# Local attention and feed-forward with other pieces: norms spread as three bf16 pieces, feed-forward from f16 halves, probabilities normalized before their transpose, v held in the array

## What is computed

```python
def attn_layer(x, Wqkv, qs, ksc, Wo):
    q, k, v = heads(x @ Wqkv)                       # 16 heads of 64
    q, k = l2norm(q) * qs, l2norm(k) * ksc
    q = q * cos * scale + rotate_half(q) * sin * scale
    k = k * cos / scale + rotate_half(k) * sin / scale
    # windows of 32 queries see their own and the window before, masked to i-32 <= j <= i
    attn = softmax(8 * q @ k.T + mask)
    return (attn @ v) @ Wo

def ffn_layer(x, g, bln, W1, b1, W2, b2):
    xn = layernorm(x) * g + bln
    a, gate = split(xn @ W1 + b1)                   # 341 and 341
    return a * gelu(gate) @ W2 + b2

for i in range(6):
    x = attn_layer(shift(x), ...) + x
    x = ffn_layer(shift(x), ...) + x
```

## Time and profile before

| | |
|---|---|
| median of 3 runs | 3942.01 us (3941.55 to 3944.91) |
| the profiled execution, its span | 3944.5 us |
| PE busy | 3691.1 us, 94% of the span |
| PEld busy | 2146.6 us, 54% |
| DVE busy | 2985.9 us, 76% |
| ACT busy | 2392.9 us, 61% |
| POOL busy | 2310.3 us, 59% |
| DMA, busy share of 16 engines | 37.4% in the queue of the data |

### The profile page before, as it was taken

How to read it: one execution, slowest core, us unless ns; L and a number is a source line. 1 busy time by engine, 2 the same in 40 slices (tenths; PEclk the granted TensorE clock), 3 DMA queues, 4 the chain that set the end, 5 groups by cost and what they waited for, 6 DMA issues and landing times.

```text
span 3944.5 us, 165118 instructions
## 1 busy us (share of the span) xinstructions
PE 3691.1 (94%) x73780; PEld 2146.6 (54%) x73780; DVE 2985.9 (76%) x3451; ACT 2392.9 (61%) x2931; POOL 2310.3 (59%) x1892
## 2 busy tenths in 40 slices
PE   7999998799999999999999999999999999999996
PEld 4666665455555555555555455555555555555553
DVE  7888886677777777777777677777777777777774
ACT  6777776455656655566555565555565656666652
POOL 4555654666655666656666565656565655666651
PEclk9999999899999999999999999999999999999998
DMA  1000001444444444445354444444444444444442
GB/s 59 5 5 7 5 5 39 106 100 111 101 101 104 108 108 104 101 95 123 89 121 95 97 103 108 108 107 96 109 112 109 101 101 103 110 103 106 101 101 77
DMA packets 162073, 349.17 MB, mean 89 GB/s; under 512 B 32606, under 2 KB 41948, under 8 KB 155100
## 3 DMA queue, kind: packets, MB, share of 16 engines
q1 hardware_dynamic: 161372, 338.62, 37.4%
HBM read 24.54 MB, written 4.19 MB: 7 GB/s over the span
## 4 chain that ended last, share of the span: by engine, by line
PE 66%; issue 5%; DMA 4%; ACT 3%; SPq 2%; DVE 2%; POOL 1%; ACTq 0%; DVEq 0%; POOLq 0%
PE psB L677 32%; PE psA L677 26%; DMA vev<-vo 3%; PE psA L732 3%; PE psB L758 2%; PE psB L732 2%; ACT pb L1015 1%; PE psA L758 1%; ACT vo L1007 1%; SPq L502 1%; SPq L486 1%; SPq L504 1%; DMA kf<-h 1%; DVE h L1253 0%; ACT sq L985 0%
## 5 line engine op out<-in xcount | busy, mean ns | idle before, releaser
L1354 POOL TENSOR_TENSOR sq<-sq 128x512 f32<-128x512 f32 x384 | 490.1, 1295 | 492.6 <-ACT sq L985 492.3
L1349 POOL TENSOR_TENSOR h<-h,ts 128x512 f32<-128x512 f32 x384 | 490.3, 1277 | 211.1 <-DVE ts L1245 211.1
L1329 POOL TENSOR_TENSOR pt<-wk,pt 128x256 f16<-128x256 f32 (+3 forms) x256 | 368.0, 1453 | 286.6 <-ACT pt L908 196.9
L1350 POOL TENSOR_TENSOR h<-h,ts 128x512 f32<-128x512 f32 x384 | 489.6, 1275 | 0.0
L985 ACT ACTIVATE sq<-psA 128x1024 f32<-128x1024 f32 x240 | 245.7, 1024 | 168.3 <-PE psA L677 168.2
L1237 DVE TENSOR_TENSOR h<-psA,t_rot 128x1024 f32<-128x1024 f32 x240 | 293.0, 1221 | 38.1 <-ACT sq L985 17.3
L677 PE MATMUL psB<-vev,ptb 64*32 64x65 f32 x9216 | 244.4, 225 | 59.0 <-ACT pb L1015 35.2
L1245 DVE TENSOR_TENSOR ts<-psA,t_rot 128x1024 f32<-128x1024 f32 x240 | 291.6, 1215 | 3.1 <-POOL h L1350 3.1
L677 PEld LDWEIGHTS psB<-vev,ptb 64*32 64x32 f32 x9216 | 194.7, 106 | 175.5 <-issue 103.3
L1364 POOL TENSOR_SCALAR f_a<-f_a 128x512 f32<-128x512 f32 x48 | 31.2, 650 | 401.6 <-DVE f_a L1293 401.6
L1253 DVE TENSOR_TENSOR h<-h,psB 128x1024 f32<-128x1024 f32 x192 | 229.5, 1217 | 42.4 <-PE psB L677 40.3
(11 more groups left out here) (343 smaller groups left out, 10637.5 us busy)
## 6 DMA issues: line engine op xcount, KB each, us to landing
qf<-h SPq DMA_DIRECT2D x768, 136.0 KB, 2.5
kf<-h SPq DMA_DIRECT2D x768, 136.0 KB
vev<-vo SPq DMA_DIRECT2D x192, 260.0 KB, 4.1
vev<-vo SPq DMA_DIRECT2D x192, 227.5 KB, 4.6
stage<-wqk SPq DMA_DIRECT2D x12, 512.0 KB, 4.6
stage<-wvl SPq DMA_DIRECT2D x12, 256.0 KB, 5.3
stage<-wof SPq DMA_DIRECT2D x6, 512.0 KB, 5.1
xb<-xt SPq DMA_DIRECT2D x8, 256.0 KB, 8.1
```

Source lines behind the costliest of these rows:

```text
L1329: e.tensor_tensor(pt[g][pr][:, :, 1, o:o + w], wk[(slot_of(s)[0] - 1) % SLOTS][:, :, 0:w], pt[g][pr][:, :, 0, o:o + w], ALU.subtract).then ...
L1349: e.tensor_tensor(halves_of(h, 0), halves_of(h, 0), t[1], ALU.subtract)
L1350: e.tensor_tensor(halves_of(h, 1), halves_of(h, 1), t[0], ALU.add).then_inc(ended["ad"])
L1354: e.tensor_tensor(sqb[c][:, 0, :], sqb[c][:, 0, :], sqb[c][:, 1, :], ALU.add).then_inc(ended["qa"])
```

## The change

It edits the local stage; the causal stage only gets its masks from another place in a table.

1. **Norms.** After nw, ACT copies n_a rounded to bf16 (ca), DVE subtracts that from groups of rows (cs), ACT copies again (cb) and DVE subtracts again (ct). Tile n_b in bf16 then holds three pieces of each norm in three groups of rows, and bc is a bf16 matmul of n_b with a `spread` that sums the three.
2. **Feed-forward.** f_c, f_g and the weights are split into high and low f16 halves. f and fo are three f16 matmuls each where they were one f32. New steps: fh (ACT) and fl (POOL) split f_c, gh (ACT) and gl (DVE) split the products. `first_halves` and `second_halves` split the weights on DVE once for each layer. The bias b2 becomes a last row of w2. The load of the next layer's weights moves from the third half of its own layer to the ninth half of the layer before.
3. **Probabilities.** DVE sums them and takes the reciprocal (sm), POOL multiplies (pn) before tp. There are two tiles for them (pbs). v loses its column of ones.
4. **pv.** v (64 columns) is loaded into the array and the transposed probabilities (32 columns) move through it. The result comes out with channels on the partitions, the kinds nm and ot are gone, and the two pv steps of an rp share one PSUM tile.
5. **Orders.** All five strings are new. `with_first` puts a few first steps ahead of the lists. The DMA scratch of GpSimd becomes 1024.

```diff
 GPSIMD = (
-    "lx qa10 ad10 qa11 qa13 qa12 ad11 xl+1 ad13 nw1 ad12 qa01+1 ad01+1 ad00+1 qa00+1 qa03+1 qa02+1 ad03+1 nw0+1 "
-    "ad02+1 "
+    "qa01 ad01 qa00 qa03 qa02 xl ad00 ad03 nw0 qa12 ad02 pn00 ad12 qa13 pn01 qa11 qa10 ad13 lx nw1 fl ad11 pn10 ad10 "
+    "pn11 "
 )
...
 TENSOR = (
...
+    "sc000:A+1 sc011+1 sc003+1 sc002+1 sc001+1 pj12:A+1 ng01+1 ng00+1 op:B bc00:B+1 vp01:A+1 vp00:A+1 bc01:B+1 la:A+1 "
+    "pj13:B+1 tp00:A+1 lb:B+1 pj11:A+1 pj10:A+1 pv000:B+1 pv001+1 tp01:B+1 ss1:A+1 fo:B sc100:B+1 pv010:A+1 sc103+1 "
+    "sc101+1 sc102+1 pv011+1 sc110:B+1 ng10+1 sc111+1 sc113+1 sc112+1 vp11:A+1 vp10:A+1 bc11:B+1 bc10:A+1 ng11+1 "
+    "pj01:A+2 tp10:B+1 f0:B+1 pv100:B+1 pv101+1 pj00:A+2 tp11:B+1 f1:A+1 pj03:B+2 pj02:B+2 f2:A+1 pv110:A+1 pv111+1 "
+    "ss0:A+2 sc010:B+2 sc013+2 sc012+2 "
...
+def with_first(steps, *first):
+
+    return list(first) + [s for s in steps if s not in first]
...
                 elif kind == "pv":
                     rp, th = s[2:]
...
+                    o = psum(("pv", v, rp, 0))
                     for tq in range(2):
-                        for x in range(2):
-                            for g in range(4):
-                                t = 2 * th + tq
-                                vals = vo[v % 2] if g % 2 else vev
+                        for g in range(4):
+                            t = 2 * th + tq
+                            vals = vo[v % 2] if g % 2 else vev
+                            for x in range(2):
                                 for q in range(2):
-                                    at = 512 * q + 65 * (2 * tq + x)
-                                    rows = slice(64 * q, 64 * q + 64)
-                                    p = mm(o[32 * g:32 * g + 32, at:at + 65], ptb[rows, x, t, 32 * g:32 * g + 32],
-                                           vals[rows, 2 * t + g // 2, 2 * rp + x, :], tile_position=(64 * q, 32 * g))
+                                    rows, at = slice(64 * q, 64 * q + 64), 512 * q + 128 * t + 32 * g
+                                    p = mm(o[64 * x:64 * x + 64, at:at + 32], vals[rows, 2 * t + g // 2, 2 * rp + x, :],
+                                           ptb[rows, x, t, 32 * g:32 * g + 32], tile_position=(64 * q, 64 * x))
...
-                        p = mm(o[:, 512 * x:512 * x + 512], spread[rows, :], n_a[rows, :], tile_position=(64 * k + 32 * x, 0))
+                        p = mm(o[:, 512 * x:512 * x + 512], spread[rows, :], n_b[rows, :], tile_position=(64 * k + 32 * x, 0))
...
-                        p = mm(o[0:n, 512 * x:512 * x + 512], w1r[:, FF * x + 128 * j:FF * x + 128 * j + n], f_c[:, :])
+                        at = FF * x + 128 * j
+                        oy = o[0:n, 512 * x:512 * x + 512]
+                        mm(oy, w1s[1][:, at:at + n], f_ch[:, :], True, False)
+                        mm(oy, w1s[0][:, at:at + n], f_cl[:, :], False, False)
+                        p = mm(oy, w1s[0][:, at:at + n], f_ch[:, :], False, True)
...
+                elif kind == "ca":
+                    e.wait_ge(*done("nw", v))
+                    e.activation(n_c[:, :], n_a[:, :], ACT.Copy).then_inc(ended["ca"])
...
+        def first_halves(e, li):
+
+            e.wait_ge(s_w1, 16 * (li + 1))
+            g = t_gs[:, li:li + 1]
+            e.tensor_scalar(w1s[0][:, :], w1r[:, :], g, None, ALU.mult).then_inc(s_w1h)
+            e.wait_ge(s_w1h, li + 1)
+            e.scalar_tensor_tensor(out=w1s[1][:, :], in0=w1r[:, :], scalar=g, in1=w1s[0][:, :], op0=ALU.mult,
+                                   op1=ALU.subtract).then_inc(s_w1s)
...
+                elif kind == "cs":
+                    e.wait_ge(*done("ca", v))
+                    e.scalar_tensor_tensor(out=n_a[:, :], in0=n_c[:, :], scalar=less[:, 0:1], in1=n_a[:, :], op0=ALU.mult,
+                                           op1=ALU.add).then_inc(ended["cs"])
...
+                elif kind == "sm":
+                    rp = s[2]
+                    if v:
+                        e.wait_ge(*done("pn", v - 1, rp))
+                    e.wait_ge(*done("ex", v, rp))
+                    e.tensor_reduce(sums[rp][:, :], pbs[rp].rearrange("p x t (f s) -> p (x t f) s", f=2), AXX, ALU.add).then_inc(s_rc)
+                    e.wait_ge(s_rc, count[s])
+                    e.reciprocal(rc[rp][:, :], sums[rp][:, :]).then_inc(ended["sm"])
...
+                elif kind == "gl":
+                    j = s[2]
+                    n = FP[j]
+                    e.wait_ge(*done("gh", v, j))
+                    e.tensor_tensor(f_gl[j][0:n, :], f_g[j][0:n, :], f_gh[j][0:n, :], ALU.subtract).then_inc(ended["gl"])
...
+                elif kind == "pn":
+                    rp = s[2]
+                    w = pbs[rp].rearrange("p x t (f s) -> p (x t f) s", f=2)
+                    e.wait_ge(*done("sm", v, rp))
+                    e.tensor_tensor(w, w, rc[rp][:, :].unsqueeze(2).to_broadcast([128, 16, 2 * W]), ALU.mult).then_inc(ended["pn"])
...
+                elif kind == "fl":
+                    e.wait_ge(*done("fh", v))
+                    e.tensor_tensor(f_cl[:, :], f_c[:, :], f_ch[:, :], ALU.subtract).then_inc(ended["fl"])
```

More of the change, by code:

```diff
@@ L27 @@
 WS = 64.0
+WF = 8.0
 TINY = WS * WS * 1e-24
@@ L242, in flat @@
             return t.rearrange("p a b -> p (a b)")
-        t_mats = sb("t_mats", [128, 384 + 160])
-        ident, center, mean, spread, heads = (t_mats[:, a:z] for a, z in ((0, 128), (128, 256), (256, 384), (384, 512),
-                                                                           (512, 544)))
-        t_masks = sb("t_masks", [128, 384 + 2 * W], BF16)
+        t_mats = sb("t_mats", [128, 384 + W + 2])
+        ident, center, mean, heads, less = (t_mats[:, a:z] for a, z in ((0, 128), (128, 256), (256, 384), (384, 416), (416, 418)))
+        t_masks = sb("t_masks", [128, 384 + 2 * W + 128], BF16)
         identb = t_masks[:, 0:128]
@@ L252, in program @@
         keyid = t_masks[:, 384:384 + 2 * W]
+        spread = t_masks[:, 384 + 2 * W:384 + 2 * W + 128]
         t_scl = sb("t_scl", [128, L, 4])
@@ L316, in program @@
         n_r, n_a = (sb("n_" + x, [128, S]) for x in "ra")
-        vo = [sb(f"vo{n}", [128, 8, 4, 65]) for n in range(2)]
-        vev = sb("vev", [128, 8, 4, 65])
-        pb = sb("pb", [128, 2, NT, 2 * 2 * W])
+        n_c, n_b = (sb("n_" + x, [128, S], BF16) for x in "cb")
+        vo = [sb(f"vo{n}", [128, 8, 4, DH]) for n in range(2)]
+        vev = sb("vev", [128, 8, 4, DH])
+        pbs = [sb(f"pb{n}", [128, 2, NT, 2 * 2 * W]) for n in range(2)]
         ptb = sb("ptb", [128, 2, NT, 128])
         negm = [sb(f"negm{n}", [128, 16], BF16) for n in range(2)]
-        rc = [sb(f"rc{n}", [128, 2, 4]) for n in range(2)]
-        ob = sb("ob", [128, 2, 2, 2, 128])
+        sums, rc = ([sb(f"{x}{n}", [128, 16]) for n in range(2)] for x in ("sum", "rc"))
         ot2 = [sb(f"ot{z}", [128, 2, 2, 2, S], F16) for z in "hl"]
@@ L326, in program @@
         f_g = [sb(f"f_g{j}", [128, S]) for j in range(3)]
+        f_ch, f_cl = (sb("f_c" + z, [128, S], F16) for z in "hl")
+        f_gh, f_gl = ([sb(f"f_g{z}{j}", [128, S], F16) for j in range(3)] for z in "hl")
+        w1s = [sb("w1" + z, [128, 2 * FF], F16) for z in "hl"]
+        w2s = [sb("w2" + z, [128, 3, 128], F16) for z in "hl"]
+        t_gs = sb("t_gs", [128, L])
         x1d = nc.dram_tensor("x1_keep", [NB, 128, S], F32).ap()
@@ L342, in program @@
         s_wa = sems("s_wa", 3)
-        s_const, s_first, s_ct, s_x, s_wo, s_wm, s_w1, s_w2, s_tab, s_stage, s_x1r = (
-            sem("s_" + n) for n in ("const", "first", "ct", "x", "wo", "wm", "w1", "w2", "tab", "stage", "x1r"))
+        s_const, s_first, s_cin, s_x, s_wo, s_wm, s_w1, s_w2, s_tab, s_stage, s_x1r = (
+            sem("s_" + n) for n in ("const", "first", "cin", "x", "wo", "wm", "w1", "w2", "tab", "stage", "x1r"))
         s_dm = sems("s_dm", 4)
@@ L508, in sync @@
                     heads_of(e, li + 1, 0)
-                if u == 2 and li:
-                    e.wait_ge(*all_done("f", *((NB * li - 1, j) for j in range(3))))
-                    e.wait_ge(*done("fo", NB * li - 1))
-                    feed_of(e, li)
+                if u == 8 and li + 1 < L:
+                    e.wait_ge(*done("lb", NB * li))
+                    e.wait_ge(s_w1s, li + 1)
+                    e.wait_ge(s_w2s, li + 1)
+                    feed_of(e, li + 1)
             e.wait_ge(*done("ss", 2 * NB * L - 1))
@@ L1038, in local_scalar @@
                     if v:
-                        e.wait_ge(*all_done("f", *((v - 1, j) for j in range(3))))
+                        e.wait_ge(*done("fl", v - 1))
                     e.wait_ge(*done("la", v))
@@ L1055, in local_scalar @@
                     if v:
+                        e.wait_ge(*done("gl", v - 1, j))
+                    e.activation(f_g[j][0:n, :], psum(("f", v, j))[0:n, 512:1024], ACT.Gelu, bias=b1s[0:n, 3 + j:4 + j],
+                                 scale=1.0 / WF).then_inc(ended["ge"])
```

(15 more changed lines are left out.)

183 lines of the change are left out of this document (96 added, 87 removed), and 15 rows, old and new, of tables (SCALAR, TENSOR, VECTOR).

## The result

The changed kernel takes 4086.34 us (median of 4 runs, 4081.37 to 4093.41) where the kernel before took 3941.78 beside it (3938.24 to 3944.91): a ratio of 1.037, 95% interval 1.0354 to 1.0386. It is slower by 145 us. Of that some 130 us lie in the repeated blocks, 2.4 to 2.8 us in each of 48. The rest stands ahead of them: the first addition of the attention to x (line 1276 before, 1318 after) starts at 810.7 us where it started at 792.6, and from the first to the last of them pass 3238.7 us where 3111.4 passed. The forecast was 3760 us, its range ended at 3910, and its sign was wrong.

What follows compares the result with a forecast made beforehand. PE's own work was taken as the bound before. After, DVE at 58.4 us a block would be longest; with 4.4 of waits 62.8, 3.9 less in 48 blocks, plus 3 for the start: 3760 us, range over cases 3570 to 3910.

Steps and rivals of the forecast that it cites:

- PE's own work back to back: Local stage before: PE busy 63.6 us of a 66.7 us block, so what shortens PE shortens the block.
- a spread of the norms: PE's bc steps: four of 1.06 us become bf16 steps of 0.25, 3.3 us less a block.
- A pair of pv: Two steps of the weighted sum of v on PE, each near 1.15 us; 2.8 us more a block.
- Rival C: PE's pv steps: loads of v go one by one, 1.8 us a step, 3882 us in all; chance 0.12.
- 56.7 forecast: PE's work in a block after the change, down from 63.6 us, between 53.9 and 59.2.
- 58.4, 56.2 and 45.0 forecast: Busy us a block after the change on DVE, POOL and ACT, from 50.4, 40.5 and 40.0.
- The product pn: POOL's multiplication of the probabilities, four a block at 2.55 us each, 10.2 us more.
- The mutual holding of DVE and POOL: Shared SBUF ports lengthen seven DVE instructions (cs, ct, gl): 4.5 us a block on DVE, 4.4 on POOL.
- With no slack I take 4.4: Waits of the longest engine, DVE at 58.4 us: 4.4 us a block, making 62.8.
- the start, put at 3 us: First splits of the weights stand ahead of DVE's walk: 3 us once.
- D: Probabilities reach PE's transposes late by way of DVE and POOL: block 70.0 us, 4103 us, slower; chance 0.12.
- A: The forecast: DVE and POOL become the bound through each other, 60.8 to 64.5 us a block, 3670 to 3845; chance 0.46.

Runs made afterwards that it cites:

- e13: The kernel before with the output projection by its high halves alone, 8 of 24 matmuls: 3869.93 us (ratio 0.9821).
- e14: The kernel before with v and the transposed probabilities in one f16 piece instead of f32: 3825.42 us (ratio 0.9704).
- e5: The kernel before with only the feed-forward by f16 halves put into its old order: 3991.19 us (ratio 1.0137).
- e8: The kernel before with only the norms spread as three bf16 pieces, put into its old order: 4010.97 us (ratio 1.018).
- e10: The kernel before with both the bf16 norms and the f16 feed-forward, put into its old order: 4120.36 us (ratio 1.0465).
- e9: The kernel after with GpSimd's multiplication of the probabilities cut to 16 of 1024 columns: 4060.21 us (ratio 1.029).
- e16: The kernel after with DVE's row sums of the probabilities over 4 of 16 groups only: 4077.47 us (ratio 1.0354).
- e12: The kernel after with v and the transposed probabilities in single f16, 512 instructions a block fewer: 3834.07 us (ratio 0.9724).
- e17: e12 with DVE's row sums of the probabilities over 4 of 16 groups only: 3777.28 us (ratio 0.958).
- the bare row: The kernel before with 512 small f32 matmuls in one row, without waits, ahead of its local stage: 3960.13 us against 3939.96.
- e1: The kernel after with only PE's order changed, large steps put between the small ones in both rows: 4386.42 us (ratio 1.1141).

## Why the prediction was wrong

**What bounds the kernel before.** Read as PE's own work back to back, with the next engine 13 us away. Wrong in its weight: the share passed on is 0.42 (e13) to 0.55 (e14), and work of other engines in the wrong place costs time at once (e5, e8, e10). An engine busy for 95% of a stretch need not be the bound of the next edit; waits of 0.7 us by 36 blocks may have been the sign of a cycle through several engines that is nearly as long; no run measured that cycle.

**The sizes on PE.** Good. f16 matmuls follow each other by 0.215 us (2521.44, 2521.66), and a spread of the norms takes 0.32, not 0.25. A pair of pv takes 2.00 us (2522.83 to 2524.83), 1.00 a step against 0.79 before and 1.15 forecast: +1.7 us a block for +2.8. Rival C, with loads one by one at 1.8 us a step, did not show. The Trainium skill, page "TensorE: Matmul & The Clock Gate", section "Part 3: Packing small matmuls — row/col tiling", states that a load overlaps matmuls only where its row group differs; the 1.79 us that the forecast made of it are not what the trace shows, and no run tests the rule itself. In all 56.7 forecast, 58.1 measured. But some 3 us of the 58.1 are the lower clock (the estimate above), which the forecast did not have: it left the granted clock where it was, at 0.99. At the upper level PE's work would be some 55 us, under the forecast.

**The sizes on DVE, POOL, ACT.** 58.4, 56.2 and 45.0 forecast, 57.0, 51.6 and 43.7 measured. The product pn takes 2.11 us, not 2.55. The mutual holding of DVE and POOL is real: of the 144 low halves gl (line 1350) the 20 with no GpSimd instruction at their side took 679 ns in the mean and the other 124 took 1251; line 1293 lasts 685 to 1860 ns, line 1299 660 to 1608, and POOL's additions of line 1398 take 1393 ns where the same ones took 1277 before (line 1349 there). The Trainium skill, page "SBUF — State Buffer", section "SBUF: two separate sides", has this rule, and the durations agree. What it costs in time was small where a run touched it: 26 us (e9, with n_b and the last gl short), 9 us (e16). No run made all seven instructions short, so its whole cost stays open; at 679 ns each they would take 4.8 us a block and take 8.3.

**The step that failed: the waits.** "With no slack I take 4.4" was the wait of the longest engine. The longest is PE with 58.1 us, not DVE with 57.0, and it waits 11.0 us a block. 6.8 of the 11.0 are PE's instruction supply, which the prediction has nowhere, though the order was there to be read: two pv, ss and eight sc in a row are some 800 instructions, and the earlier trace rows gives the pace, 96 records in 1.17 us. What it could not give was the rate of supply: the kernel before has issue waits of 4.0 us at most and 1.3 a block. The remaining 4.2 us are waits for n_b, xb, ts, negm: strict order. Two smaller terms failed as well: the lower clock, put at nothing, is worth some 2.6 us a block more than before by the estimate above, and the start, put at 3 us, took 18.

**The rivals.** D came nearest in time, 4103 us, for a cause that is not there: no transpose waits for POOL. A right number from a wrong mechanism is no merit. A comes near for e12, which has fewer instructions in its rows: 62.8 us a block forecast, 64.0 there, with DVE at 57.2 and PE waiting for DVE's n_b, ts and f_g. That is in part luck: pv is cheaper there than the forecast had it, 3.2 us a block of issue waits remain, and e17 shows that DVE does not set the block.

**What stays open.** How far the old order's cycle could be shortened by other places for the new steps; what the first 18 us are; what idle time brings the lower clock, which no run varied by itself (the bare row did its second portion, after a pause of 1.86 us, still at the upper level, and e1 had more of the lower level with a third of the issue waits); and why portions come at 3.3 to 4.1 us when a transfer itself takes about 1.

## What to carry to other kernels

Count instructions, not only time, in each stretch of a matrix engine's list: here more than some 256 in 3.5 us, held for longer than what is already fetched, made it run dry, and averages over a block hid it. Idle time in such a list can cost twice, here by a lower clock for what follows (8.0 us a block). Before moving to smaller or split pieces, ask what they add to the densest row. Adding the busy times of engines gave each sum within 5 us and the time with the wrong sign; in a strict list the price of an edit is whom it makes late, and one run that takes work from the supposed bound (here 70 of 166 us came back) tells that before anything is built.
